# Moving small steps inside an engine's program: chain work, a cast, and long GpSimd additions in a fused attention and feed-forward kernel

## The chip, the core and the metric

The kernel runs on one core of a Trainium2 chip. The core has five engines that run their own instruction streams and wait for each other through semaphores: TensorE (PE, matrix products and transposes into PSUM), VectorE (DVE), ScalarE (ACT), GpSimd (POOL) and SyncE (SP, which issues the transfers). The metric is the device time of one execution in microseconds; lower is better.

## The reference, cut to what matters

The input x has 4 batches of 2048 rows of 256. Four residual layers follow each other, each on a layer norm of x:

```python
x = x + attn_a(layernorm(x))   # linear attention, 16 heads of 16, bias
x = x + ffn(layernorm(x))      # shared expert: square(relu(z @ Ws1)) @ Ws2, plus routed experts
x = x + attn_b(layernorm(x))   # iterated softmax over the first 16 positions of each batch
x = x + ffn(layernorm(x))
```

In `attn_a`, q and k pass through elu + 1, `kv = k^T v` is summed over a whole batch, and `out = (q kv) / max(q . sum(k), 1e-6)`. In `attn_b` only the first 16 rows of each batch attend (64 rows in all, three iterations with a test for an early end); every other row gets the bias `ob` alone. The routed part of `ffn` is weighted by the truncated softmax of two values, which is zero unless the router weights are very large, so the kernel guards it with a flag that is off for these inputs.

## The kernel before

All rows are cut into 16 groups of 512 (4 tiles of 128). **Pass 1** (up to about 182 us of the span) normalises each group, forms k and q in split precision (high and low fp32r halves) and sums `kv` for each batch. **Pass 2** is a software pipeline of 18 steps, written out by hand for each engine in a function `step(g, b)`. In step i three groups are in work at once: group i gets the attention, group r = i - 1 the first feed-forward layer, group v = i - 2 the second. The program order of each engine, and nothing else, decides what runs next; an instruction that waits holds up all that stands behind it on its engine.

The names used from here on, in the order of TensorE's step before the change, with their lines:

- **W** (L1539): q times kv and Wo, 16 products into PA. VectorE adds the result to x (**W add**, L1071).
- **bc** (L1407): spreads 1/normalizer of group i + 1 over its heads into PB; VectorE multiplies q by it (**q_scale**, L956). It reads `n_op`, written by VectorE (**n_split**, L949).
- **f1** (L1557): first layer's hidden product of group r; ScalarE squares its relu (L751, L753).
- **f4** (L1522): output product of the second layer, group v. VectorE adds two of its tiles to x, each scaled by its row's 1/variance (**scaled_sum**, L1059); ScalarE scales the other two (L738), and GpSimd adds them (**y3 add**, L549).
- **r2** (L1571): spreads the inverse variances of group r over columns of PT. VectorE makes them (L1049, one reciprocal for groups r and v together) from what GpSimd prepared (`four_variances`, L494 to L501) from VectorE's `bn_stats` (**x_stats**, L1038).
- **T2** (L1577): transposes of group i.
- **f3** (L1586): hidden product of the second layer. It reads `h2s`, the product of the squared relu and r2's columns, made by VectorE (**h2s**, L1095).
- **n** (L1398): normalizer of group i + 2. VectorE takes it out of PSUM (L939), inverts it (L941) and casts it to its high half (L943, `n_hi`); n_split makes the operand with the low half.
- **f2** (L1522 again): output product of the first layer; VectorE adds it to x (**f2 add**, L1104), after GpSimd has added the rows `ob` there (**ob add**, L455).

The 64 special rows of `attn_b` are carried along as a serial **chain** of small pieces, `chain(i, slot)`, with slots 1, 2 and 3 at fixed places of each engine's step. Most pieces pass a result from one engine to the next.

Of the kernel before, what the change touches and what calls it, by code (L numbers as in the profile page):

```python
# [44 lines left out]
def hybrid_kernel(nc, x_in, Wq, bq, Wk, bk, Wv, bv, Wo, bo, qw, qb, kw, vw, vb, ow, ob,  # L45
# [18 lines left out]
    with ExitStack() as ctx:  # L64
# [16 lines left out]
        minus_low = sb("minus_low", [P, 1])  # L81
# [165 lines left out]
        bn3, var3, rsq = sem("bn3"), sem("var3"), sem("rsq")  # L247
# [9 lines left out]
        n_mm, n_taken, n_inv, n_op_done = [sem(n) for n in ("n_mm", "n_taken", "n_inv", "n_op_done")]  # L257
# [73 lines left out]
        def _(sp):  # L331
# [74 lines left out]
            sp.wait_ge(stored, 16 * (NG - 1))  # L406
# [9 lines left out]
        def _(pool):  # L416
# [114 lines left out]
            def step(g, b):  # L531
                i = g * B + b
                r, nr, _ = lagged(g, b, 1)
                v, nv, _ = lagged(g, b, 2)
                if runs(r):
# [3 lines left out]
                ge(pool, rsq, i - 1)  # L539
                if runs(v):  # L540
                    four_variances(1, v, bn3, var3)
# [20 lines left out]
        def _(act):  # L562
# [40 lines left out]
            def pass1(b, last):  # L603
                for g in range(G):
# [5 lines left out]

                    ge(act, q_done, n)
# [121 lines left out]
            def scale_tiles(i, v):  # L733
                act.wait_ge(f4_mm, v + 1)
                act.wait_ge(rsq, i)
# [5 lines left out]
            def step(g, b):  # L741
# [4 lines left out]
                if i == 0:  # L746
                    fold_ffn()
                if runs(r):
# [7 lines left out]
                chain(i, 1)  # L756
# [8 lines left out]
                chain(i, 2)  # L765
                if i <= NG:
                    run_experts(i, r)
# [16 lines left out]
        def _(dve):  # L784
# [45 lines left out]
            nc.vector.memset(minus_low[:, :], -1.0).then_inc(sel_ready, 1)  # L830
# [40 lines left out]
            def pass1(b, last):  # L871
                for g in range(G):
# [4 lines left out]

                    ge(dve, g_mm, n)
# [11 lines left out]
                    if last and g == G - 1:  # L890
                        dve.wait_ge(sel_ready, 2 + T + 1)
                        n_take(0)
                        n_split(0)
# [9 lines left out]
                    if isinstance(n, int) and n == 2:  # L903
                        dve.wait_ge(sel_ready, 2)
                        for t in range(T):
                            nc.vector.memset(minus_low[t * 2 * H:t * 2 * H + H, :], 0.0).then_inc(sel_ready, 1)
                        by_half = ident[:, :].rearrange("p (t u k o) -> p t u k o", t=T, u=2, o=1)
                        nc.vector.tensor_tensor(sel[:, :, :].rearrange("p k f -> p (k f)").rearrange("p (t k e) -> p t k e", t=T, e=HD),
                                                by_half[:, :, 0, :, :].to_broadcast([P, T, H, HD]),
                                                by_half[:, :, 1, :, :].to_broadcast([P, T, H, HD]), ALU.add).then_inc(sel_ready, 1)  # L910
# [25 lines left out]
            def n_take(j):  # L936
# [5 lines left out]
                dve.wait_ge(n_inv, 2 * j + 1)  # L942
                nc.vector.tensor_copy(n_hi[:, :], n_sb[:, :]).then_inc(n_inv, 1)  # L943

            def n_split(j):

                dve.wait_ge(n_inv, 2 * j + 2)
# [92 lines left out]
            def reciprocal_variances(i, r, v):  # L1040

                slots = slice(0 if runs(r) else 1, 2 if runs(v) else 1)
                if runs(r):
                    dve.wait_ge(var2, 5 * (r + 1))
                    ge(dve, r2_mm, r)
                if runs(v):
                    dve.wait_ge(var3, 5 * (v + 1))
                    ge(dve, f4_scaled, 2 * v)
                nc.vector.reciprocal(ln_rsq[:, slots, :], ln_a[:, slots, :]).then_inc(rsq, 1)  # L1049

            def scaled_sum(i, v, nv):
# [3 lines left out]
                dve.wait_ge(rsq, i)  # L1055
# [6 lines left out]
            def step(g, b):  # L1062
# [3 lines left out]
                j, nj, _ = lagged(g, b, -1)  # L1066
                if runs(i):
# [13 lines left out]
                if i > 0:  # L1081
                    reciprocal_variances(i, r, v)
# [4 lines left out]
                if runs(v):  # L1087
                    scaled_sum(i, v, nv)
                chain(i, 1)
                if runs(r):  # L1090
# [4 lines left out]
                    nc.vector.tensor_tensor(h2s, h2, PT[:, 1, :], ALU.mult).then_inc(f1_scaled, 1)  # L1095
                chain(i, 2)
                if runs(i + 2):
                    n_take(i + 2)
                chain(i, 3)
# [5 lines left out]
                if runs(i + 2):  # L1105
                    n_split(i + 2)
                if runs(r):
# [163 lines left out]
        def _(pe):  # L1271
# [138 lines left out]
            def pass1(b, last):  # L1410
                for g in range(G):
# [3 lines left out]
                    if last and g == G - 1:  # L1415
                        n_product(0, 0, 0)
# [108 lines left out]
            def step(g, b):  # L1525
# [22 lines left out]
                if runs(j):  # L1548
                    ge(pe, f2_added, i - 1)
                    bc_product(j, PB)  # L1550
                if runs(r):
# [13 lines left out]
                chain(i, 1)  # L1565
                if runs(r):
                    pe.wait_ge(rsq, i)
                    pe.wait_ge(n_taken, min(i + 2, NG))
                    ge(pe, f1_scaled, r)
                    for t in range(T):  # L1570
                        last = nc.tensor.transpose(PT[:, 1, t * P:(t + 1) * P], ln_rsq[:, 0, t:t + 1].to_broadcast([P, P]), ident[:, :])  # L1571
                    last.then_inc(r2_mm, 1)
# [10 lines left out]
                chain(i, 2)  # L1583
# [5 lines left out]
                chain(i, 3)  # L1589
                if runs(r):  # L1590
# [5 lines left out]
                    down(PB, h2s, f2_mm)  # L1596
                if i <= NG:
# [162 lines left out]
```

## Time and profile before

| what | value |
|---|---|
| time, median of 3 runs | 439.25 us (438.79 to 441.06) |
| the profiled execution, its own time | 441.03 us |
| its span, first to last instruction | 439.2 us |
| mean granted TensorE clock | 0.986 |
| busy share: PE, DVE, ACT, POOL | 92%, 71%, 47%, 49% |

The profile is of one execution. Times in it are in microseconds from the start of the span. PE's busy time is modelled for overlapping products, so the share says that PE is rarely without work, not that it runs at its peak.

### The profile page before, as it was taken

Reading aid. Unit: us, or ns where it says so; the run is one execution under the profiler, and the core shown is the slowest. Engines: PE = TensorE matmul, PEld = TensorE weight load, DVE = VectorE, ACT = ScalarE, POOL = GpSimd, SP = SyncE. Lnnn points to the kernel's source line nnn. Section 1 sums busy time; section 2 is a strip of 40 time slices with the busy share of each in tenths; the row PEclk is TensorE's granted clock in tenths of the full one; section 3 lists DMA queues with packets and bytes.
Section 4 is the critical chain, followed back from the end, with each engine's and each line's share of the span. In section 5 each row is a group of like instructions: output and inputs, shape, how many; then the busy total and the mean of one; then the engine's idle time right before and its main releaser. Section 6 shows DMA issues by size and latency. Waiting matters only on the chain.

```text
span 439.2 us, 7483 instructions
## 1 busy us (share of the span) xinstructions
PE 404.7 (92%) x2458; PEld 322.7 (73%) x2458; DVE 313.5 (71%) x654; ACT 204.5 (47%) x354; POOL 217.2 (49%) x315
## 2 busy tenths in 40 slices
PE   8898999999999998989989989999899999969983
PEld 5787889988988896777866767677666676747752
DVE  6779976576668666474667688797768877977644
ACT  3766686778778775033324422222342144223340
POOL 3675775776677664032144514662441744533630
PEclk9999999999999999899999999999999999989998
DMA  8701211111100000400011101101110110110022
GB/s 269 236 16 35 80 65 48 49 48 48 48 0 0 1 1 1 99 3 0 6 54 51 52 5 50 52 1 50 49 51 0 51 53 1 50 49 29 22 91 64
DMA packets 22982, 20.64 MB, mean 47 GB/s; under 512 B 3398, under 2 KB 22924, under 8 KB 22924
## 3 DMA queue, kind: packets, MB, share of 16 engines
q1 hardware_dynamic: 22364, 19.40, 14.1%
q8 instruction: 29, 0.48, 0.4%
q10 hardware_dynamic: 560, 0.52, 0.4%
q14 instruction: 29, 0.24, 0.2%
HBM read 11.33 MB, written 8.45 MB: 45 GB/s over the span
## 4 chain that ended last, share of the span: by engine, by line
PE 57%; DVE 18%; ACT 8%; issue 8%; POOL 7%; DVEq 1%; POOLq 0%; ACTq 0%
PE PB L1522 12%; PE PA L1539 11%; PE PT L1557 6%; PE PT L1586 4%; PE PB L1407 3%; ACT scratch L567 3%; PE PG L1358 3%; POOL ln_rstd L444 2%; DVE x_all L1059 2%; ACT scratch L614 2%; POOL ln_rstd L442 2%; DVE ln_bn L797 2%; DVE scratch L1095 2%; ACT xn_pair L578 2%; PE PT L1398 2%
## 5 line engine op out<-in xcount | busy, mean ns | idle before, releaser
L494 POOL TENSOR_TENSOR ln_a<-ln_bn 128x4 f32<-128x4 f32 x32 | 6.7, 210 | 124.2 <-DVE ln_bn L1038 124.2
L1522 PE MATMUL PB<-ws,scratch 128*128 128x256 f32 x248 | 62.3, 395 | 1.9 <-issue 1.9
L1522 PEld LDWEIGHTS PB<-ws,scratch 128*128 128x128 f32 x248 | 46.1, 195 | 20.1 <-issue 14.8
L1539 PE MATMUL PA<-kvwo,q_all 128*128 128x256 f32 x256 | 57.9, 379 | 0.0
L751 ACT ACTIVATE scratch<-PT 128x512 f32<-128x512 f32 x16 | 9.6, 598 | 102.2 <-PE PT L1557 102.2
L1539 PEld LDWEIGHTS PA<-kvwo,q_all 128*128 128x128 f32 x256 | 48.5, 190 | 6.5
L466 POOL TENSOR_TENSOR xn_pair<-scratch,xn_pair 128x1024 fp32r<-128x1024 f32 x16 | 38.5, 2406 | 20.3 <-ACT xn_pair L578 20.3
L882 DVE SCALAR_TENSOR_TENSOR scratch<-scratch,PB 128x512 f32<-128x512 f32 x32 | 20.9, 684 | 38.6 <-ACT scratch L614 38.6
L1038 DVE BATCH_NORM_STATS2 ln_bn<-x_all 128x6 f32<-128x256 f32 x128 | 44.1, 406 | 0.1
L567 ACT ACTIVATE scratch<-x_all,ln_shift,ln_rstd 128x255 f32 (+1 forms) x60 | 31.1, 593 | 22.6 <-POOL ln_shift L448 22.5
L455 POOL TENSOR_TENSOR x_all<-x_all,wvo 128x1024 f32 (+1 forms) x16 | 38.6, 2410 | 0.1
L455 POOL TENSOR_TENSOR x_all<-x_all,ob_rows 128x1024 f32<-128x1024 f32 x16 | 38.1, 2381 | 0.9 <-PE PA L1577 0.7
L1331 PE MATMUL PB<-wk_hi,xt_hi 128*128 128x256 f32 x128 | 36.9, 288 | 0.5 <-DVE xt_lo L825 0.4
L1358 PE MATMUL PG<-xn_pair,k_hi 128*128 128x512 f32 x128 | 35.2, 419 | 1.1 <-ACT k_hi L622 1.1
L1333 PE MATMUL PB<-wk_hi,xt_lo 128*128 128x256 f32 x128 | 36.2, 283 | 0.0
L1332 PE MATMUL PB<-wk_lo,xt_hi 128*128 128x256 f32 x128 | 36.2, 283 | 0.0
L1557 PE MATMUL PT<-scratch,ffn_weights 128*128 128x512 f32 x64 | 30.8, 603 | 0.0
L1104 DVE TENSOR_TENSOR x_all<-PB,x_all 128x1024 f32<-128x1024 f32 x16 | 19.5, 1221 | 15.2 <-PE PB L1522 15.2
L1586 PE MATMUL PT<-scratch,ffn_weights 128*128 128x512 f32 x32 | 18.8, 670 | 11.4 <-DVE scratch L1095 11.3
L1071 DVE TENSOR_TENSOR x_all<-PA,x_all 128x1024 f32<-128x1024 f32 x16 | 19.5, 1219 | 12.5 <-PE PA L1539 12.5
L1358 PEld LDWEIGHTS PG<-xn_pair,k_hi 128*128 128x128 f32 x128 | 24.0, 195 | 6.0 <-issue 1.3
L442 POOL TENSOR_SCALAR ln_rstd<-ln_mv 128x4 f32<-128x4 f32 x16 | 12.2, 764 | 31.4 <-DVE ln_mv L800 27.9
(252 smaller groups left out, 943.0 us busy)
## 6 DMA issues: line engine op xcount, KB each, us to landing
x_all<-n_L_attn_a_inputs_q_dram SPq DMA_DIRECT2D x15, 512.0 KB, 3.6
out_dram<-x_all SPq DMA_DIRECT2D x15, 512.0 KB, 3.2
out_dram<-x_all SPq DMA_DIRECT2D x2, 256.0 KB, 2.2
x_all<-n_L_attn_a_inputs_q_dram SPq DMA_DIRECT2D x2, 128.0 KB, 3.0
x_all<-n_L_attn_a_inputs_q_dram ACTq DMA_DIRECT2D x2, 128.0 KB, 3.4
setup<-in_L_attn_a_Wk_dram SPq DMA_DIRECT2D x1, 256.0 KB, 4.9
setup<-in_L_attn_a_Wq_dram ACTq DMA_DIRECT2D x1, 256.0 KB, 5.1
wvo<-in_L_attn_a_Wv_dram SPq DMA_DIRECT2D x1, 256.0 KB, 6.4
```

The source lines that it names most:

```text
L455: nc.gpsimd.tensor_tensor(x_group(n), x_group(n), rows_[:, :].rearrange("p (o d) -> p o d", o=1).to_broadcast([P, T, D]), ALU.add).then_in ...
L466: nc.gpsimd.tensor_tensor(xn_pair[:, :, 1, :], xn[g % 2], xn_pair[:, :, 0, :].bitcast(F32), ALU.subtract).then_inc(x_lo, 1)
L567: nc.scalar.activation(dst[:, t:t + 1, 0:width], x_tile(n, t)[:, :, 0:width], ACT.Identity, scale=ln_rstd[:, slot, t:t + 1], bias=ln_shift ...
L1038: nc.vector.bn_stats(ln_bn[:, slot, t:t + 1, :], x_tile(n, t)).then_inc(bn, 1)
L1331: mm(dst, hi, wk_hi[:, c, :], start=(c == 0), stop=False)
L1332: mm(dst, hi, wk_lo[:, c, :], start=False, stop=False)
L1333: last = mm(dst, lo, wk_hi[:, c, :], start=False, stop=(c == C - 1))
L1358: mm(PG[:, c, :], k_hi[:, t, c * P:(c + 1) * P], xn_pair[:, t, :, :].rearrange("p h d -> p (h d)"), start=(g == 0 and t == 0), stop=False, ...
L1522: last = mm(four(pair)[:, t, :], h[:, t * P:(t + 1) * P], ws2[:, :], start=True, stop=True)
L1539: last = mm(four(PA)[:, t, :], q_all[:, n * C + c, t * P:(t + 1) * P], kvwo[:, b * C + c, :], start=(c == 0), stop=(c == C - 1))
L1557: last = mm(PT[:, 0, :], w1c[:, c, :], x2t[:, c, :], start=(c == 0), stop=(c == C - 1))
L1586: mm(PT[:, 0, :], wc, h2s, start=False, stop=True, skip_group_check=True).then_inc(f3_mm, 1)
```

## The change

The change reorders the steps of pass 2 and a little of pass 1, and moves one cast between engines.

- TensorE: slot 1 of the chain and r2 go ahead of f1; slot 2 goes ahead of T2 (from step 2 on); slot 3 goes behind f2. The normalizer product of group 0 goes ahead of the last group's k product in pass 1.
- VectorE: the reciprocal is cut in two, for group r ahead of the W add, and for group v behind q_scale. Slot 1 goes ahead of x_stats, h2s ahead of scaled_sum, slot 3 behind n_split. The cast to `n_hi` leaves VectorE.
- ScalarE: makes `n_hi` (`n_high`), ahead of the second layer's relu. Slot 1 goes ahead of the first layer's relu.
- GpSimd: the y3 add is one step later (group u = i - 3), and it and the ob add stand at the head of the step, behind a wait for the normalizer product of the step before.
- SyncE: the store of a finished group is one step later too.

```diff
@@ SyncE step
+                u, nu, _ = lagged(g, b, 3)
+                if runs(u):
+                    sp.wait_ge(out_dve, 2 * (u + 1))
+                    sp.wait_ge(out_pool, u + 1)
+                    sp.dma_start(out_dram[bass.ds(nu, 1)].rearrange("o p t d -> p (o t) d"), x_group(nu)).then_inc(stored, 16)
...
-                elif runs(v):
-                    sp.wait_ge(out_dve, 2 * (v + 1))
-                    sp.wait_ge(out_pool, v + 1)
-                    sp.dma_start(out_dram[bass.ds(nv, 1)].rearrange("o p t d -> p (o t) d"), x_group(nv)).then_inc(stored, 16)
...
-            sp.wait_ge(stored, 16 * (NG - 1))
+            sp.wait_ge(stored, 16 * (NG - 2))
@@ GpSimd step
+                if runs(r):
+                    pool.wait_ge(n_mm, min(i + 2, NG))
+                if runs(u):
+                    pool.wait_ge(f4_scaled, 2 * (u + 1))
+                    last = x_all[:, nu * T + 2:(nu + 1) * T, :]
+                    nc.gpsimd.tensor_tensor(last, last, y3, ALU.add).then_inc(out_pool, 1)
...
-                if runs(v) and v < NG - 1:
-                    pool.wait_ge(f4_scaled, 2 * (v + 1))
-                    last = x_all[:, nv * T + 2:(nv + 1) * T, :]
-                    nc.gpsimd.tensor_tensor(last, last, y3, ALU.add).then_inc(out_pool, 1)
@@ ScalarE
+            def n_high(j):
+
+                act.wait_ge(n_inv, j + 1)
+                ge(act, n_op_done, j)
+                nc.scalar.activation(n_hi[:, :], n_sb[:, :], ACT.Copy).then_inc(n_hi_done, 1)
...
+                if runs(i + 2):
+                    n_high(i + 2)
@@ VectorE
-                dve.wait_ge(n_inv, 2 * j + 1)
-                nc.vector.tensor_copy(n_hi[:, :], n_sb[:, :]).then_inc(n_inv, 1)
...
-                nc.vector.scalar_tensor_tensor(n_op[:, :], n_hi[:, :].bitcast(F32), minus_low[:, 0:1], n_sb[:, :],
-                                               ALU.mult, ALU.add).then_inc(n_op_done, 1)
+                nc.vector.scalar_tensor_tensor(n_op[:, :], n_sb[:, :], low_row[:, 0:1], n_hi[:, :].bitcast(F32),
+                                               ALU.mult, ALU.subtract).then_inc(n_op_done, 1)
...
+                if runs(r):
+                    reciprocal_variances(0, r, var2, r2_mm, rsq)
...
-                if i > 0:
-                    reciprocal_variances(i, r, v)
+                if runs(v):
+                    reciprocal_variances(1, v, var3, f4_scaled, rsq3)
+                chain(i, 1)
@@ TensorE
+                if isinstance(n, int) and n == NG - 1:
+                    n_product(0, 0, 0)
```

The selection matrix `sel` changes sign to fit the new `n_op`. Three places of the new order follow. The first is VectorE in step 13, from the W add to the f2 add; the rows L1236 to L1242 are the chain's slot 1, L1247 its slot 2 and L1250 its slot 3. Before:

```order
L1071 TENSOR_TENSOR x_all<-PA,x_all 128x1024
L956 TENSOR_TENSOR q_all<-q_all,PB 128x1024
L1049 RECIPROCAL ln_rsq<-ln_a 128x8
L1038 BN_STATS ln_bn<-x_all 128x6 x4
L1059 SCALAR_TENSOR_TENSOR x_all<-PB,ln_rsq,x_all 128x256 x2
L1236 TENSOR_REDUCE b_weights<-q_all 128x16
...
L1242 TENSOR_SCALAR b_weights<-b_weights,q_all 128x256
L1095 TENSOR_TENSOR scratch<-scratch,PT 128x512
L1247 TENSOR_TENSOR b_weights<-PG,b_weights 128x256
L939 TENSOR_SCALAR n_sb<-PT 128x128
L941 RECIPROCAL n_sb<-n_sb 128x128
L943 CAST n_hi<-n_sb 128x128
```

And the same stretch of the changed program, where L1103 is h2s, L1067 scaled_sum, L1051 x_stats and L1246 to L1252 slot 1:

```order
L1057 RECIPROCAL ln_rsq<-ln_a 128x4
L1081 TENSOR_TENSOR x_all<-PA,x_all 128x1024
L969 TENSOR_TENSOR q_all<-q_all,PB 128x1024
L1057 RECIPROCAL ln_rsq<-ln_a 128x4
L1246 TENSOR_REDUCE b_weights<-q_all 128x16
...
L1252 TENSOR_SCALAR b_weights<-b_weights,q_all 128x256
L1051 BN_STATS ln_bn<-x_all 128x6 x4
L1103 TENSOR_TENSOR scratch<-scratch,PT 128x512
L1067 SCALAR_TENSOR_TENSOR x_all<-PB,ln_rsq,x_all 128x256 x2
L1257 TENSOR_TENSOR b_weights<-PG,b_weights 128x256
L954 TENSOR_SCALAR n_sb<-PT 128x128
L956 RECIPROCAL n_sb<-n_sb 128x128
```

h2s stood behind scaled_sum and slot 1; now slot 1 stands ahead of x_stats, and scaled_sum behind h2s. The second place is TensorE in step 7, from bc to f2; L1660 is the chain's slot 1 and L1602 its slot 3. Before:

```order
L1407 MATMUL PB<-n_op,sel 128x128 x8
L1557 MATMUL PT<-scratch,ffn_weights 128x512 x2
L1522 MATMUL PB<-ws,scratch 128x256 x4
L1660 MATMUL PG<-q_all,scratch 128x256 x4
L1571 MATMUL PT<-ident,ln_rsq 128x128 x4
L1577 MATMUL PA<-ident,x_all 128x128 x8
L1586 MATMUL PT<-scratch,ffn_weights 128x512
L1398 MATMUL PT<-q_all,kmask 32x128 x8
L1602 MATMUL PG<-ident,q_all 128x128 x2
L1522 MATMUL PB<-ws,scratch 128x256 x4
```

And after, with L1673 and L1615 for the two chain pieces, L1567 for r2, L1575 for f1, L1599 for f3 and L1410 for n:

```order
L1419 MATMUL PB<-n_op,sel 128x128 x8
L1673 MATMUL PG<-q_all,scratch 128x256 x4
L1567 MATMUL PT<-ident,ln_rsq 128x128 x4
L1575 MATMUL PT<-scratch,ffn_weights 128x512 x2
L1532 MATMUL PB<-ws,scratch 128x256 x4
L1589 MATMUL PA<-ident,x_all 128x128 x8
L1599 MATMUL PT<-scratch,ffn_weights 128x512
L1410 MATMUL PT<-q_all,kmask 32x128 x8
L1532 MATMUL PB<-ws,scratch 128x256 x4
L1615 MATMUL PG<-ident,q_all 128x128 x2
```

Slot 1 and r2 moved from behind f4 to the place ahead of f1, and slot 3 from ahead of f2 to the end of the step. The third place is the end of pass 1 on TensorE, where the k product of the last group is 24 rows L1331 to L1333 (L1343 to L1345 after) and the q product begins with L1346 (L1358 after). Before:

```order
L1358 MATMUL PG<-xn_pair,k_hi 128x512 x8
L1363 MATMUL PG<-xn_pair,k_lo 128x256 x8
L1331 MATMUL PB<-wk_hi,xt_hi 128x256
L1332 MATMUL PB<-wk_lo,xt_hi 128x256
L1333 MATMUL PB<-wk_hi,xt_lo 128x256
...
L1398 MATMUL PT<-q_all,kmask 32x128 x8
L1346 MATMUL PA<-xt_hi,wq_hi 128x512
```

And after:

```order
L1370 MATMUL PG<-xn_pair,k_hi 128x512 x8
L1375 MATMUL PG<-xn_pair,k_lo 128x256 x8
L1410 MATMUL PT<-q_all,kmask 32x128 x8
L1343 MATMUL PB<-wk_hi,xt_hi 128x256
L1344 MATMUL PB<-wk_lo,xt_hi 128x256
L1345 MATMUL PB<-wk_hi,xt_lo 128x256
...
L1358 MATMUL PA<-xt_hi,wq_hi 128x512
```

The normalizer product of group 0 moved from behind the last k product to the place ahead of it.

## Rows read from the trace of the kernel before

**Rows 1.** Page, busy time and share of the span, by engine.

```profile
PE 404.7 (92%) x2458; PEld 322.7 (73%) x2458; DVE 313.5 (71%) x654; ACT 204.5 (47%) x354; POOL 217.2 (49%) x315
```

**Rows 2.** Chain that ended last, step 4: start us, us, engine, tile, line.

```profile
239.70 3.45 PE PA L1539 x16
243.15 0.84 PE PB L1407 x8
243.99 1.77 PE PT L1557 x4
245.76 1.86 PE PB L1522 x8
...
247.64 0.88 DVE x_all L1059 x2
248.52 0.60 DVE scratch L1095
...
249.17 1.12 PE PT L1586 x2
250.29 0.57 PE PT L1398 x16
250.87 1.92 PE PB L1522 x8
252.79 3.45 PE PA L1539 x16
```

**Rows 3.** Waits of PE, whole span: us in total, times, longest us.

```profile
PE PT L1586 <- DVE scratch L1095: 11.3, 11, 3.4
PE PT L1407 <- DVE n_op L949: 2.6, 1, 2.6
PE PB L1522 <- issue: 1.9, 4, 0.7
...
PE PG L1602 <- ACT q_all L704: 1.5, 1, 1.5
...
PE PB L1407 <- DVE n_op L949: 1.0, 3, 0.4
...
PE PG L1638 <- ACT b_weights L690: 0.6, 1, 0.6
```

**Rows 4.** Windows: stretch, length, busy per engine, granted clock, DMA share, GB/s.

```profile
177.40:181.00 3.60, 3.60 (x11) 2.82 (x11) 1.29 (x2) 0.00 (x0) 0.00 (x0) 0.53 0.18 1
...
389.00:391.90 2.90, 2.89 (x18) 0.99 (x18) 0.29 (x1) 0.85 (x2) 0.00 (x0) 0.52 0.00 0
...
426.70:430.10 3.40, 3.40 (x10) 2.68 (x9) 0.00 (x0) 1.32 (x2) 0.00 (x0) 0.50 0.48 158
...
437.00:438.00 1.00, 0.00 (x0) 0.00 (x0) 0.00 (x0) 0.00 (x0) 0.00 (x0) 0.50 0.99 327
```

**Rows 5.** Timeline of DVE, step 11 and step 13: start, length, instruction.

```profile
346.66 1.31 DVE L949 SCALAR_TENSOR_TENSOR n_op<-n_hi,minus_low,n_sb 128x128 fp32r<-128x128 f32 x1
...
386.02 2.21 DVE L1242 TENSOR_SCALAR b_weights<-b_weights,q_all 128x256 f32<-128x256 f32 x1
```

**Rows 6.** Timeline of POOL, the same two stretches.

```profile
345.28 2.54 POOL L455 TENSOR_TENSOR x_all<-x_all,ob_rows 128x1024 f32<-128x1024 f32 x1
...
384.50 1.28 POOL L549 TENSOR_TENSOR x_all<-x_all,scratch 128x512 f32<-128x512 f32 x1 [0.30 <-ACT scratch L738]
385.73 2.35 POOL L455 TENSOR_TENSOR x_all<-x_all,ob_rows 128x1024 f32<-128x1024 f32 x1
```

**Rows 7.** Timeline of ACT, a 128x128 activation from SBUF to SBUF.

```profile
418.60 0.31 ACT L715 ACTIVATE q_all<-q_all 128x128 f32<-128x128 f32 x1
```

**Rows 8.** Page, costliest groups: busy us, mean ns of one, idle before.

```profile
L751 ACT ACTIVATE scratch<-PT 128x512 f32<-128x512 f32 x16 | 9.6, 598 | 102.2 <-PE PT L1557 102.2
...
L1038 DVE BATCH_NORM_STATS2 ln_bn<-x_all 128x6 f32<-128x256 f32 x128 | 44.1, 406 | 0.1
...
L1071 DVE TENSOR_TENSOR x_all<-PA,x_all 128x1024 f32<-128x1024 f32 x16 | 19.5, 1219 | 12.5 <-PE PA L1539 12.5
```

More of the change, by code:

```diff
@@ L256, in hybrid_kernel @@
         kvwo_mm, kvwo_done, sel_ready = [sem(n) for n in ("kvwo_mm", "kvwo_done", "sel_ready")]
-        n_mm, n_taken, n_inv, n_op_done = [sem(n) for n in ("n_mm", "n_taken", "n_inv", "n_op_done")]
+        n_mm, n_taken, n_inv, n_hi_done, n_op_done = [sem(n) for n in ("n_mm", "n_taken", "n_inv", "n_hi_done", "n_op_done")]
         bc_mm, q_scaled, w_mm, w_added = [sem(n) for n in ("bc_mm", "q_scaled", "w_mm", "w_added")]
@@ L609, in pass1 @@
                     x_high(n, g)
+                    if last and g == G - 1:
+                        n_high(0)
                     ge(act, q_done, n)
@@ L746, in step @@
                 if i == 0:
+                    n_high(1)
                     fold_ffn()
+                chain(i, 1)
                 if runs(r):
@@ L755, in step @@
                     scale_tiles(i, v)
-                chain(i, 1)
                 if runs(i):
@@ L876, in pass1 @@
                         copy_g(b - 1)
+                    if last and g == G - 1:
+                        dve.wait_ge(sel_ready, 2 + T + 1)
+                        n_take(0)
+                        n_split(0)
                     ge(dve, g_mm, n)
@@ L889, in pass1 @@
                     nc.vector.tensor_tensor(k_lo[:, :, :], k_tok, k_hi[:, :, :].bitcast(F32), ALU.subtract).then_inc(k_lo_done, 1)
[L890 to L893, printed above, removed]
                     if not (last and g == G - 1):
@@ L905, in pass1 @@
                         for t in range(T):
-                            nc.vector.memset(minus_low[t * 2 * H:t * 2 * H + H, :], 0.0).then_inc(sel_ready, 1)
+                            nc.vector.memset(low_row[t * 2 * H:t * 2 * H + H, :], 0.0).then_inc(sel_ready, 1)
                         by_half = ident[:, :].rearrange("p (t u k o) -> p t u k o", t=T, u=2, o=1)
                         nc.vector.tensor_tensor(sel[:, :, :].rearrange("p k f -> p (k f)").rearrange("p (t k e) -> p t k e", t=T, e=HD),
-                                                by_half[:, :, 0, :, :].to_broadcast([P, T, H, HD]),
-                                                by_half[:, :, 1, :, :].to_broadcast([P, T, H, HD]), ALU.add).then_inc(sel_ready, 1)
+                                                by_half[:, :, 1, :, :].to_broadcast([P, T, H, HD]),
+                                                by_half[:, :, 0, :, :].to_broadcast([P, T, H, HD]), ALU.subtract).then_inc(sel_ready, 1)
                     if last and g == G - 1:
@@ L1038, in x_stats, with reciprocal_variances @@
                     nc.vector.bn_stats(ln_bn[:, slot, t:t + 1, :], x_tile(n, t)).then_inc(bn, 1)
[L1040 to L1049, printed above, removed]
+            def reciprocal_variances(slot, j, ready, used, done):
+                dve.wait_ge(ready, 5 * (j + 1))
+                ge(dve, used, j if slot == 0 else 2 * j)
+                nc.vector.reciprocal(ln_rsq[:, slot, :], ln_a[:, slot, :]).then_inc(done, 1)
             def scaled_sum(i, v, nv):
@@ L1054, in scaled_sum @@
                 dve.wait_ge(f4_mm, v + 1)
-                dve.wait_ge(rsq, i)
+                dve.wait_ge(rsq3, v + 1)
                 if v < B:
@@ L1080, in step @@
                     q_scale(j, nj, PB)
-                if i > 0:
-                    reciprocal_variances(i, r, v)
+                if runs(v):
+                    reciprocal_variances(1, v, var3, f4_scaled, rsq3)
+                chain(i, 1)
                 if runs(i):
@@ L1086, in step @@
                     x_stats(n, 0, bn2)
-                if runs(v):
-                    scaled_sum(i, v, nv)
-                chain(i, 1)
                 if runs(r):
@@ L1095, in step @@
                     nc.vector.tensor_tensor(h2s, h2, PT[:, 1, :], ALU.mult).then_inc(f1_scaled, 1)
+                if runs(v):
+                    scaled_sum(i, v, nv)
                 chain(i, 2)
@@ L1098, in step @@
                     n_take(i + 2)
-                chain(i, 3)
                 if runs(r):
@@ L1106, in step @@
                     n_split(i + 2)
+                chain(i, 3)
                 if runs(r):
@@ L1414, in pass1 @@
                     k_product(n, g, b)
-                    if last and g == G - 1:
-                        n_product(0, 0, 0)
                     if isinstance(n, int) and n == 0:
@@ L1550, in step @@
                     bc_product(j, PB)
+                chain(i, 1)
+                if runs(r):
+                    pe.wait_ge(rsq, r + 1)
+                    pe.wait_ge(n_taken, min(i + 2, NG))
+                    ge(pe, f1_scaled, r)
+                    for t in range(T):
+                        last = nc.tensor.transpose(PT[:, 1, t * P:(t + 1) * P], ln_rsq[:, 0, t:t + 1].to_broadcast([P, P]), ident[:, :])
+                    last.then_inc(r2_mm, 1)
                 if runs(r):
@@ L1564, in step @@
                     down(PB if v < NG - 1 else PA, h3, f4_mm)
[L1565 to L1572, printed above, removed]
+                if i > 1:
+                    chain(i, 2)
                 if runs(i):
@@ L1582, in step @@
                     pe.wait_ge(kvwo_done, B)
-                chain(i, 2)
+                if i <= 1:
+                    chain(i, 2)
                 if runs(r):
@@ L1588, in step @@
                     n_product(jj, njj, bjj)
-                chain(i, 3)
                 if runs(r):
@@ L1596, in step @@
                     down(PB, h2s, f2_mm)
+                chain(i, 3)
                 if i <= NG:
```

13 lines of the change are left out of this document (7 added, 6 removed).

## The prediction

> **What bounds the kernel.** I read the busy shares first: PE is busy for 92% of the span [rows 1], so what can be won is PE's idle time and the time that PE runs at the lower clock. Next comes the chain that ended last, in an ordinary step without chain work [rows 2]. W, bc, f1 and f4 follow each other on PE; then the chain leaves PE for scaled_sum (0.88) and h2s (0.60) and comes back to PE for f3, n and f2. From one W start to the next it is 252.79 - 239.70 = 13.09 us. f4 ends at 247.62 and f3 starts at 249.17, a hole of 1.55 us which r2 and T2 fill but for 0.25. By their counts, 4 and 8 transposes, these take about 0.44 and 0.87. An ordinary step is thus 12.84 us of PE work. Then I read who makes PE wait [rows 3]: h2s for 11.3 us at 11 places, of which 3.4 at one; n_op for 2.6 at the end of pass 1 and 1.0 at three places after; f4, four times and 1.9 in all, put down to "issue", which I take for its wait on q_scale; a chain piece on ScalarE for 1.5. Last, the clock: behind the long waits the windows show a granted clock of 0.53, 0.52 and 0.50, the lower level of 1.2 GHz, for some 3 us each [rows 4].
>
> **Why VectorE is late.** At 386.02 a VectorE instruction on SBUF operands takes 2.21 us and ends 0.15 us after GpSimd's ob add, which runs from 385.73 to 388.08; n_split at 346.66 takes 1.31 us and ends at 347.97, with GpSimd's addition ending at 347.82 [rows 5, 6]. So a VectorE instruction whose operands are all in SBUF stands still until a long GpSimd addition has ended. Additions with a PSUM operand beside it keep their length (W adds average 1.22 over all steps) [rows 8].
>
> **The change, part by part.** I write E for the end of W and lay out a new ordinary step from these durations. PE: bc to E+0.84, r2 to 1.28, f1 to 3.05, f4 to 4.91, T2 to 5.78, f3 to 6.90, n to 7.47, f2 to 9.39; the next E is 12.84 [rows 2]. VectorE: W add and q_scale (1.2 each) to E+2.5, reciprocal, x_stats (44.1 us for 128, so 1.4 for four) to about 4.0. f1's square is ready 1.45 us after f1 (two activations of 0.60 and gaps), at 4.5, so h2s ends at 5.2 [rows 2, 8]. f3 wants to start at 5.78, so **its wait is gone, with 0.6 us to spare**. The cast on ScalarE costs about 0.31 [rows 7]. It holds the second relu back until after the inversion, but that result is wanted only by f4 of the next step, over 5 us later.
>
> GpSimd starts behind n, at 7.47: y3 add 1.28 and ob add 2.35 end at about 11.2 [rows 6]. n_split wants to start at 10.7, behind the f2 add, so it is held in every step, to about 11.6; x_stats then ends at 12.9 and the next reciprocal at 13.1, where r2 wants it at 12.84 + 0.84 = 13.7. The hold costs nothing as long as it grows by less than 0.6 us.
>
> 1. **End of pass 1.** n_op is ready while PE is in the q product, so bc does not wait: 2.6 us [rows 3]. The stretch behind it, 177.4 to 181, ran at 0.53 [rows 4], and 3.6 x 0.47 = 1.7 us goes too if PE keeps busy. What is late next is the last group's q_scale, and it gives W a wait of about 0.2. I take **4.1** (2.6 if the clock drops all the same; 4.3).
> 2. **h2s waits, 11.3 us** [rows 3]. The chain's slot 1 (three to six operations on 256 columns or fewer; at x_stats's 0.34 to 0.41 each I estimate 1.0 to 1.8 us) now lies ahead of x_stats, and only what goes beyond the 0.6 us shows: 0.4 left in step 2 and 0.5 in step 13. In step 16, which has no W, T2 or n as cover, 1.4 us of wait stays or changes place. I take **9.0** (5.6 if step 13 keeps its 3.4; 10.4).
> 3. **Clock behind step 13's wait**: 2.9 x 0.48 = **1.4** [rows 4] (0 to 1.4).
> 4. **bc and q_scale waits**, 0.6 of the 1.0 and the 1.9 [rows 3]. They came from chain work and held casts between n and the next W. Two slot 3 pieces (the softmax in steps 10 and 12, three operations on 256 columns, estimated at 0.41 each as x_stats's [rows 8], 1.3 us with links) still delay the W add of the next step, by 0.35 and 0.2. Gain **1.9** (1.2 to 2.5).
> 5. **Step 8's wait of 1.5** for the softmax's exp: slot 3 on PE is now behind f2, and the held subtraction ahead of it runs before GpSimd starts. **1.5** (1.0 to 1.7).
> 6. **Step 1 loses.** Its chain piece stood between f1 and T2 and covered the path f1, square, h2s (1.45 + 0.60 + 0.05 = 2.1). Now only T2's 0.87 covers it, which is 1.25 us of new wait; the 0.6 for L1638 goes [rows 3]. **-0.65** (-0.3 to -1.0).
> 7. **Step 0 loses** about **0.4**: n_high stands ahead of ScalarE's fold copies, for which bc waits (0 to -0.6).
> 8. **Step 16: 0** (+1.5 to -1.5). r2 now precedes f1, and the reciprocal for it stands behind the f2 add and x_stats (1.2 + 1.35): PE starts f1 about 2.9 us later than before. It saves r2's and part of f3's later waits. Before, f2 of this step ran at 0.50 [rows 4]. If the clock falls in the new hole, this is lost again; if not, 1 us or so is won.
> 9. **End of the kernel.** The store of group 14 (512 KB) used to be out before the last two halves. Now it is issued behind the four small output stores, just ahead of those halves. At the 327 GB/s that the last store reached [rows 4] 512 KB is 1.6 us; a part of it passes before the first half is ready. **-1.2** (0 to -1.6).
>
> On the last term, the Trainium skill, DMA: Bandwidth & Descriptors, section Queues, rings and completion order, says that each DMA engine takes descriptors of one issuer's ring in order; by that the halves queue behind the late store and the whole 1.6 us would show. No row of the trace before has two large stores together.
>
> Sum: 4.1 + 9.0 + 1.4 + 1.9 + 1.5 - 0.65 - 0.4 + 0 - 1.2 = **15.65 us**. The profiled execution took 441.03 (span 439.2) and would take 425.4. It lies 1.8 us above the median of the runs shown; from the median 439.25 I get **423.6 us**.
>
> **Rivals.**
>
> *VectorE becomes the bound.* In every step n_split stands behind both long GpSimd additions. Were GpSimd 1 us later than I place it (its own additions were stretched where VectorE was busy in SBUF: 2.54 against 2.35 [rows 6]), the reciprocal would come at 14.1 where r2 wants it at 13.7, and each of 13 steps would lose 0.4 to 0.5, some 6 us: 429.6. For it: slack is only 0.6. Against: n's removal of the cast frees VectorE, and no other pure SBUF instruction falls under the additions. The Trainium skill, SBUF - State Buffer, section SBUF: two separate sides, has a rule that speaks so: VectorE, with two SBUF inputs, and GpSimd take a shared port pair for a whole instruction, whichever comes first, and the other stands still. By that rule the hold can go either way.
>
> *Step 13 keeps its wait.* Its six chain operations still precede h2s. If they are held as at 386.02, terms 2 and 3 lose 3.4 + 1.4: 428.4. Against: in the new order GpSimd has only short operations there.
>
> *Slower.* r2 is now ahead of f1, and every piece of PE's step is behind it. If VectorE's reciprocal came later than E+0.84 by more than (15.65 + 2.2)/13 = 1.4 us in each of 13 steps, the change would cost over 2 us: about 443. That needs the held n_split to end 2 us later than I place it, which only a GpSimd that starts late could do.
>
> *The change does not do what it says*: waits reappear one for one at the moved places, as in terms 6 to 9. Then about 438 to 440.
>
> **Chances.** My forecast with its small variations, 417.5 to 427: 0.67. VectorE bound: 0.14. Step 13 keeps its wait: 0.10. No change: 0.03. Slower: 0.06. The likeliest is 423.6; the range reaches from term bounds at the low side (all good ends give some 21 us, 418 to 419) to both middle rivals with a little more, 418.5 to 431. A difference of 0.5%, about 2.2 us, is what these runs can tell from none. Faster by more than that 0.91, within it 0.03, slower 0.06.
>
> **What would show it.** PE's waits for h2s fall from 11.3 to under 4 us. bc has no wait at the end of pass 1, and W first starts near 177.7. Ordinary steps come every 12.85 us; step 13 takes about 14.6, and the granted clock is 1.00 all through it. n_split is long (0.8 or more) in most steps while its cast is gone. A wait of 1.2 for h2s appears in step 1, one of 2 to 3 us ahead of r2 in step 16. The last store lands some 1.2 us later behind the last scaled_sum. I am wrong if r2 waits in ordinary steps, or if new chain waits stand ahead of f1.

## The result and the profile after

The changed kernel takes **417.05 us** (median of 4 runs, 414.62 to 417.81) against 439.04 us for the kernel before, measured beside it (4 runs). The ratio is 0.948, 95% interval 0.943 to 0.953. Ratios here and below leave out runs that are more than 1.5% above the fastest of the same kernel. The direction and the mechanism were forecast, the size was not: 423.6 us was predicted with a range of 418.5 to 431.0, and the time lies below it. The profiled execution took 417.81 us with a span of 416.1, so it gained 23.1 us of span where the sum said 15.65. Between the medians the gain is 22.0; the profiled execution of the kernel before took 2.0 more than its median here.

I read PE's waits first, as [rows 3] were read: us in total, times, longest.

```profile
PE PT L1599 <- DVE scratch L1103: 1.2, 1, 1.2
...
PE PT L1567 <- DVE ln_rsq L1057: 1.0, 1, 1.0
PE PB L1419 <- ACT ffn_weights L733: 0.8, 1, 0.8
PE PG L1741 <- ACT q_all L727: 0.7, 1, 0.7
```

f3's wait for h2s has fallen from 11.3 us at 11 places [rows 3] to 1.2 at one, the one forecast in step 1. Of the others, r2 (L1567) and the chain piece L1741 wait in step 16, and bc (L1419) in step 0. In steps 2 to 14 no wait is shown any more. Next, PE's timeline of one ordinary step, step 4 (start us, length, instruction). It is best read by the distance from one start to the next, since the lengths overlap.

```profile
233.30 3.62 PE L1549 MATMUL PA<-kvwo,q_all 128*128 128x256 f32 x16
236.57 1.19 PE L1419 MATMUL PB<-n_op,sel 128*128 128x128 f32 x8
237.60 0.62 PE L1567 MATMUL PT<-ident,ln_rsq 128*128 128x128 f32 x4
238.05 1.88 PE L1575 MATMUL PT<-scratch,ffn_weights 128*128 128x512 f32 x4
239.77 1.89 PE L1532 MATMUL PB<-ws,scratch 128*128 128x256 f32 x8
241.50 1.04 PE L1589 MATMUL PA<-ident,x_all 128*128 128x128 f32 x8
242.37 1.02 PE L1599 MATMUL PT<-scratch,ffn_weights 128*128 128x512 f32 x2
243.32 0.64 PE L1410 MATMUL PT<-q_all,kmask 128*32 128x128 f32 x16
243.90 1.99 PE L1532 MATMUL PB<-ws,scratch 128*128 128x256 f32 x8
245.73 0.81 PE L1549 MATMUL PA<-kvwo,q_all 128*128 128x256 f32 x3
```

The step takes 245.73 - 233.30 = 12.43 us; I had forecast 12.84. The same view of the kernel before, from f1 to n of step 4, with VectorE's q_scale beside it, shows where that 0.4 us lay:

```profile
243.83 1.93 PE L1557 MATMUL PT<-scratch,ffn_weights 128*128 128x512 f32 x4
...
244.33 1.21 DVE L956 TENSOR_TENSOR q_all<-q_all,PB 128x1024 f32<-128x1024 f32 x1
...
245.64 1.96 PE L1522 MATMUL PB<-ws,scratch 128*128 128x256 f32 x8
247.44 0.60 PE L1571 MATMUL PT<-ident,ln_rsq 128*128 128x128 f32 x4
247.88 1.04 PE L1577 MATMUL PA<-ident,x_all 128*128 128x128 f32 x8
249.17 1.12 PE L1586 MATMUL PT<-scratch,ffn_weights 128*128 128x512 f32 x2 [0.25 <-DVE scratch L1095]
250.22 0.64 PE L1398 MATMUL PT<-q_all,kmask 128*32 128x128 f32 x16
```

From start to start, before and after: f1 to what follows 1.81 and 1.72; f4 to what follows 1.80 and 1.73; T2 to f3 1.29 and 0.87; f3 to n 1.05 and 0.95. The sum of the differences is 0.09 + 0.07 + 0.42 + 0.10 = 0.68, the whole gain of the step (13.10 to 12.43, within rounding). The idle time that the row shows is 0.25.

By the first W product of each step in the two traces, the gain lies here (us):

| stretch | before | after | gain | predicted |
|---|---|---|---|---|
| start to the first W | 181.76 | 177.40 | 4.36 | 4.1 |
| steps 0 and 1 | 29.97 | 30.89 | -0.92 | -1.05 |
| steps 2 to 12 and 14 | 175.30 | 161.38 | 13.92 | 8.5 |
| step 13 | 19.91 | 13.78 | 6.13 | 5.3 |
| step 15 to the end | 32.26 | 32.65 | -0.39 | -1.2 |

The prediction's terms are not given by step: 5.3 is 19.91 less the 14.6 forecast for step 13, and 8.5 is what the sum leaves beside the other rows. Most of the 7.5 us that were missed is thus in the steady steps, in which PE does the same work in another order.

### The profile page after: what moved, and what is told of

Same layout as the page of the kernel before. It is cut to its first block, busy times and chain, and to the rows that moved or that the text cites. A ratio compares the mean times of both kernels' runs of the same rounds, so it can differ in the third digit from the quotient of the medians.

```text
span 416.1 us, 7524 instructions
## 1 busy us (share of the span) xinstructions
PE 396.5 (95%) x2458; PEld 320.4 (77%) x2458; DVE 307.3 (74%) x653; ACT 207.7 (50%) x370; POOL 216.6 (52%) x315
## 4 chain that ended last, share of the span: by engine, by line
PE 65%; DVE 9%; ACT 8%; POOL 7%; issue 7%; DMA 1%; DVEq 1%; POOLq 0%; ACTq 0%; SPq 0%
PE PB L1532 13%; PE PA L1549 13%; PE PT L1575 6%; PE PT L1599 4%; PE PA L1589 3%; ACT scratch L571 3%; PE PB L1419 3%; PE PG L1370 3%; POOL ln_rstd L445 2%; POOL ln_rstd L443 2%; DVE ln_bn L812 2%; PE PT L1410 2%; ACT scratch L620 2%; ACT xn_pair L582 2%; PE PT L1567 2%
## 5 line engine op out<-in xcount | busy, mean ns | idle before, releaser
L1532 PE MATMUL PB<-ws,scratch 128*128 128x256 f32 x248 | 60.5, 387 | 0.0
L1051 DVE BATCH_NORM_STATS2 ln_bn<-x_all 128x6 f32<-128x256 f32 x128 | 44.5, 409 | 0.2
L1343 PE MATMUL PB<-wk_hi,xt_hi 128*128 128x256 f32 x128 | 37.0, 289 | 0.5 <-DVE xt_lo L840 0.4
L1345 PE MATMUL PB<-wk_hi,xt_lo 128*128 128x256 f32 x128 | 36.2, 283 | 0.0
L1370 PE MATMUL PG<-xn_pair,k_hi 128*128 128x512 f32 x128 | 33.7, 405 | 1.1 <-ACT k_hi L628 1.1
L1575 PE MATMUL PT<-scratch,ffn_weights 128*128 128x512 f32 x64 | 31.5, 616 | 0.0
L542 POOL TENSOR_TENSOR x_all<-x_all,scratch 128x512 f32<-128x512 f32 x15 | 19.0, 1268 | 21.2 <-PE PT L1410 14.9
L1370 PEld LDWEIGHTS PG<-xn_pair,k_hi 128*128 128x128 f32 x128 | 23.1, 188 | 5.6 <-issue 1.3
```

The source lines that it names most:

```text
L1051: nc.vector.bn_stats(ln_bn[:, slot, t:t + 1, :], x_tile(n, t)).then_inc(bn, 1)
L1343: mm(dst, hi, wk_hi[:, c, :], start=(c == 0), stop=False)
L1345: last = mm(dst, lo, wk_hi[:, c, :], start=False, stop=(c == C - 1))
L1370: mm(PG[:, c, :], k_hi[:, t, c * P:(c + 1) * P], xn_pair[:, t, :, :].rearrange("p h d -> p (h d)"), start=(g == 0 and t == 0), stop=False, ...
L1532: last = mm(four(pair)[:, t, :], h[:, t * P:(t + 1) * P], ws2[:, :], start=True, stop=True)
L1575: last = mm(PT[:, 0, :], w1c[:, c, :], x2t[:, c, :], start=(c == 0), stop=(c == C - 1))
```

## The experiments

The theory after the result (A): a wait of PE costs more than its idle time in the trace, and a wait shorter than the end of the products before it shows no idle time at all. The main rival (B): r2's new place is in itself the shorter order. The edits below are shortened; a name such as h2s or r2 stands for its lines.

**VectorE's order undone alone.** In the changed kernel:

```diff
-                h2s (waits f1_sq, r2_mm)
                 if runs(v):
                     scaled_sum(i, v, nv)
+                h2s (waits f1_sq, r2_mm)
```

> The changed kernel, with h2s put back behind scaled_sum on VectorE and nothing else undone. Theory A (a wait of PE costs more than the idle time that the trace shows beside it: about 0.17 us of the products before it still count as busy, and the first product behind it takes 0.10 longer): f3 waits for h2s again in nearly every step, the start of T2 to the start of f3 grows from 0.87 to about 1.8 us while the wait shown is 0.6 to 0.7, f3 to n grows from 0.95 to 1.05, and a step takes 13.4 instead of 12.43; time 428 to 431. Rival B (what was under-sized is the gain of r2's new place ahead of f1): f3's wait comes back with what the row shows and no more, a step takes about 13.0, time 423 to 425.

Measured: 426.68 us, ratio to before 0.970 (0.965 to 0.974). Timeline of an ordinary step; PEld is the weight load.

```profile
243.62 1.04 PE L1589 MATMUL PA<-ident,x_all 128*128 128x128 f32 x8
...
245.35 0.30 PEld L1599 LDWEIGHTS PT<-scratch,ffn_weights 128*128 128x128 f32 x2 [0.93 <-DVE scratch L1105]
245.35 1.12 PE L1599 MATMUL PT<-scratch,ffn_weights 128*128 128x512 f32 x2 [0.69 <-DVE scratch L1105]
...
246.41 0.64 PE L1410 MATMUL PT<-q_all,kmask 128*32 128x128 f32 x16
```

T2 to f3 is 1.73 (0.87 without the wait), f3 to n 1.06 (0.95), and the step is 13.38. The wait costs 0.96 where the row shows 0.69. The two missing parts can be seen. T2 counts as busy for 1.04 us though f3 follows it after 0.87 when nothing waits, so 0.17 of a wait lies under it. And the weight load starts together with the product that waited; in the changed kernel it starts at 242.26, 0.11 ahead of its product at 242.37:

```profile
242.26 0.30 PEld L1599 LDWEIGHTS PT<-scratch,ffn_weights 128*128 128x128 f32 x2
```

The Trainium skill, TensorE: Matmul & The Clock Gate, section Step-by-step: what each phase is for, says that weight loads are pulled ahead of running products and that the end of one product overlaps the beginning of the next, which one standing alone can't use. The trace agrees where nothing waits; ahead of the waiting product the load was not pulled ahead. The total came 1.3 us below my 428, since the chain's steps lose less (some of their pieces already fill the hole).

**PE's order undone alone.** r2 back behind f4, in the changed kernel:

```diff
                 chain(i, 1)
-                r2 (waits rsq, n_taken)
                 f1
                 f4
+                r2 (waits rsq, n_taken)
                 if i > 1:
                     chain(i, 2)
```

> The changed kernel, with r2 alone put back behind f4 on PE (ahead of T2). Theory A: h2s is still ahead of scaled_sum and is ready when T2 ends, so f3 waits for little or nothing; the starts of f1, f4, r2 and T2 stay 1.72, 1.73 and 0.45 apart, a step takes 12.4 to 12.6 and the time is 416 to 420; step 16, where r2 no longer waits ahead of f1, gains 1 to 2 us. Rival B (r2's place made the ordinary step shorter): f1 to f4 is 1.81 and f4 to r2 1.80 as before the change, a step takes 12.8 or more, time 421 or more.

Measured: 418.14 us, 0.950 (0.945 to 0.954): 1.1 above the changed kernel, which the intervals don't separate. But the ordinary step takes 12.81 with no wait shown, as B said, and A's numbers for it were wrong; the time lies in A's range (416 to 420) and not in B's (421 or more). Timeline of one:

```profile
238.34 1.93 PE L1568 MATMUL PT<-scratch,ffn_weights 128*128 128x512 f32 x4
...
238.84 1.21 DVE L969 TENSOR_TENSOR q_all<-q_all,PB 128x1024 f32<-128x1024 f32 x1
...
240.15 1.97 PE L1532 MATMUL PB<-ws,scratch 128*128 128x256 f32 x8
...
241.95 0.60 PE L1581 MATMUL PT<-ident,ln_rsq 128*128 128x128 f32 x4
...
242.39 1.04 PE L1589 MATMUL PA<-ident,x_all 128*128 128x128 f32 x8
...
242.65 0.69 DVE L1103 TENSOR_TENSOR scratch<-scratch,PT 128x512 f32<-128x512 f32 x1 [1.22 <-issue]
...
243.39 1.13 PE L1599 MATMUL PT<-scratch,ffn_weights 128*128 128x512 f32 x2
```

q_scale ends at 240.05 and f4 starts 0.10 behind it, where f1 alone would have let it start at 238.34 + 1.72 = 240.06. h2s ends at 243.34 and f3 starts at 243.39, where T2 would have let it start at 243.26. Both are waits of about 0.1 without idle time in the trace. That made a second form of A: r2's place matters only since it shifts f4 away from q_scale and brings h2s forward. (That the total hardly moves: step 1 is shorter by 0.43, and the stretch from step 15's W to the end, with f1 of step 16 no longer behind r2's wait, by 2.1.)

**r2 issued twice** tells this second form from B: four more transposes ahead of f1 on top of the last kernel.

```diff
                 chain(i, 1)
+                r2 (the same four transposes to PT, without its count)
                 f1
                 f4
                 r2
```

> The kernel of the run with r2 behind f4, which issues r2 a second time ahead of f1 (the same four transposes to the same place; work is added, none is left out). It shifts f1 and f4 by 0.45 without moving r2. Theory A, second form (the place of r2 matters only because f4 came 0.1 us after q_scale's end and f3 0.1 after h2s: waits that show no idle time since the products before them still drain): f1 to f4 falls from 1.81 to 1.72, f4 to r2 from 1.80 to 1.73, and an ordinary step takes 12.85 to 13.0. Rival B (r2 behind f4 is in itself the slower order): both stay at 1.81 and 1.80, and a step takes 13.25.

Measured: 423.94 us (one run). One of its ordinary steps:

```profile
239.60 1.88 PE L1574 MATMUL PT<-scratch,ffn_weights 128*128 128x512 f32 x4
241.32 1.89 PE L1532 MATMUL PB<-ws,scratch 128*128 128x256 f32 x8
243.05 0.60 PE L1587 MATMUL PT<-ident,ln_rsq 128*128 128x128 f32 x4
```

f1 to f4 is 1.72 and f4 to r2 1.73 with r2 still behind f4: B falls. The step takes 13.10, above my 12.85 to 13.0, because h2s still waits for the late r2: T2 to f3 stays at 1.00 and f3 to n at 1.05. 12.43 + 0.44 for the transposes + 0.13 + 0.10 is 13.10.

Since a copy of r2 stands ahead of f1 in this run too, it leaves open whether f1 and f4 are shorter only behind r2. The trace of the kernel before answers that in step 15, which has no bc and no q_scale:

```profile
410.39 1.88 PE L1557 MATMUL PT<-scratch,ffn_weights 128*128 128x512 f32 x4
412.11 1.89 PE L1522 MATMUL PB<-ws,scratch 128*128 128x256 f32 x8
413.83 0.60 PE L1571 MATMUL PT<-ident,ln_rsq 128*128 128x128 f32 x4
```

f1 to f4 and f4 to r2 are 1.72 each, with r2 behind f4 and none of it ahead of f1.

**h2s first, in the kernel before**, one part of the change alone:

```diff
+                h2s (waits f1_sq, r2_mm)
                 scaled_sum(i, v, nv)
                 chain(i, 1)
-                h2s (waits f1_sq, r2_mm)
```

> The kernel before, with h2s ahead of scaled_sum and of the chain's slot 1 on VectorE, and nothing else of the change. Theory A: that swap alone takes away the wait of the ordinary steps with what it really costs (0.67 us in a step where 0.25 is shown) and the 3.4 of step 13 with the half clock behind it: an ordinary step takes 12.45 to 12.65, time 424 to 428. Rival B (it takes r2's place, the spread slots or GpSimd's new order as well): a step stays above 12.8, step 13 keeps a wait over 2 us, time 431 or more.

Measured: 441.33 us (median of 10 runs, 437.21 to 444.50), ratio 1.002 (0.999 to 1.006): nothing. Its waits of PE:

```profile
PE PG L1602 <- DVE q_all L1155: 2.8, 1, 2.8
...
PE PG L1602 <- DVE q_all L1215: 2.2, 2, 1.1
PE PB L1407 <- DVE n_op L949: 2.0, 2, 1.6
```

The ordinary step is 12.81 (steps 2 and 4; 13.36 in step 3), B's figure, and step 13 has lost its wait, as A had it. But A's time was far off. h2s waits for r2 behind f4, slot 1 and all of VectorE's later work waits with it, and PE then stands ahead of the chain pieces and of bc: the waits at L1602 add up to 11.8 us, as much as the 11.3 for h2s before.

**Slot 1 undone alone**, in the changed kernel on VectorE:

```diff
-                chain(i, 1)
                 x_stats(n, 0, bn2)
                 h2s
                 scaled_sum(i, v, nv)
+                chain(i, 1)
```

> The changed kernel with VectorE's chain slot 1 alone put back behind scaled_sum (h2s stays ahead of both; PE's slots stay as changed). Theory A (the slots had to move with h2s: PE's piece between f4 and T2, wanted 8.2 to 9 us after the step's start, reads what VectorE's slot 1 makes, which then ends 2 us or more later): in six or seven of the steps 5 to 14 PE waits 1 to 3 us ahead of that piece, ordinary steps stay at 12.43; time 424 to 431. Rival B (h2s ahead of scaled_sum and r2 ahead of f1 carry the gain alone, the spread slots are worth little): chain steps grow by less than 0.3 each, time 416.5 to 420.

Measured: 434.08 us, 0.983 (0.978 to 0.988): 17 us worse than the changed kernel (15 by the ratios to the kernel before), more than A's 424 to 431. Ordinary steps stay at 12.43.

```profile
PE PG L1615 <- DVE b_weights L1267: 2.5, 1, 2.5
...
PE PG L1615 <- DVE q_all L1200: 2.2, 1, 2.2
```

PE waits 1.5 to 2.5 us ahead of a chain piece in six steps (6, 8, 9, 10, 12 and 15), and behind the 2.2 the granted clock fell: 0.66 from 273 to 278, which makes step 6 19.72 long. So h2s's place pays only together with slot 1's: here PE's pieces of the chain stand at their new places, and VectorE makes what they read too late.

**The end of pass 1 alone**, in the kernel before: the product, take and split of group 0's normalizer early (the diff of the change).

> The kernel before, with the first n product, its take and its split ahead of the last group of pass 1 and nothing else. By the trace after the change this is worth 4.4 us (the first W started at 177.40 instead of 181.76): W first starts at 177.3 to 177.8 and the time is 434 to 435.5. Rival: the rest needs the cast on ScalarE, and W starts at 179 or later, time 436.5 or more.

Measured: 437.74 us, 0.996 (0.993 to 0.998). The first W starts where I said, but the time is above my 434 to 435.5. The window (granted clock in the third column from the end) shows a loss in step 2 of the profiled execution:

```profile
177.23 3.69 PE L1539 MATMUL PA<-kvwo,q_all 128*128 128x256 f32 x16 [1.19 <-DVE q_all L956]
```

```profile
219.60:223.60 4.00, 4.00 (x25) 3.12 (x25) 1.47 (x3) 1.32 (x2) 0.43 (x1) 0.57 0.20 64
```

Behind the same wait of 1.87 for h2s in step 2 the clock fell here, and step 2 took 16.34 instead of 14.71; in the trace of before it stayed at 1.00 behind a wait of 1.86 (223.0 to 226.4). But from step 15's W on this execution took 30.60 us instead of 32.29, so that against the trace of before the whole 4.5 is left (a span of 434.7 for 439.2). The medians, 437.74 and 439.65, differ by 1.9; what the other executions lost, and where, no trace shows.

**The cast back on VectorE**, in the changed kernel:

```diff
                 nc.vector.reciprocal(n_sb, n_sb).then_inc(n_inv, 1)
+                nc.vector.tensor_copy(n_hi, n_sb).then_inc(n_hi_done, 1)
@@ ScalarE
-                n_high(i + 2)
```

> The changed kernel with the cast of n back on VectorE, between the reciprocal and the f2 add, instead of on ScalarE. Theory A (a VectorE cast on SBUF operands stands still under GpSimd's additions, which now start right behind n): the cast takes 1 to 2.5 us instead of 0.25, the f2 add, x_stats and the W add behind it come 1 us or more later, f4 waits for q_scale in ordinary steps; a step takes 12.8 to 13.6, time 422 to 432. Rival B (the cast slips in between the two additions, or its delay is hidden): steps stay at 12.4 to 12.5, time 416.5 to 418.5.

Measured: 424.48 us, 0.966 (0.964 to 0.968). An ordinary step takes 13.17:

```profile
232.79 2.35 POOL L456 TENSOR_TENSOR x_all<-x_all,ob_rows 128x1024 f32<-128x1024 f32 x1
232.83 2.39 DVE L953 CAST n_hi<-n_sb 128x128 fp32r<-128x128 f32 x1
...
238.06 0.65 PE L1564 MATMUL PT<-ident,ln_rsq 128*128 128x128 f32 x4 [0.22 <-DVE ln_rsq L1054]
```

The cast (0.25 by itself) stands until the ob add has ended, the f2 add behind it starts at 235.14 instead of 233.50, and bc, r2 and f4 wait (f1 to f4 takes 1.80 again). A is borne out.

**GpSimd's additions at their old places**, in the changed kernel (the store stays one step late):

```diff
-                pool.wait_ge(n_mm, min(i + 2, NG))
-                y3 add of group u
                 add_row(nr, ob_rows, ob_added)
...
                 four_variances(0, i, bn2, var2)
+                y3 add of group v
```

> The changed kernel with GpSimd's two long additions back at their old places: ob add first thing in GpSimd's step without waiting for n, y3 add of the same step's group behind the variances. Theory A (the additions' place decides how long VectorE is held; it was needed for the gain): x_stats or n_split are held on the path, r2 or h2s comes late, time 421 or more. Rival B (with the cast gone from VectorE the old places hold nothing that PE waits for): ordinary steps stay at 12.4 to 12.5, time 415.5 to 418.5, with the store of group 14 no longer behind its late addition.

Measured: 417.46 us, 0.948 (0.944 to 0.951), the changed kernel's time, and 12.43 an ordinary step. n_split is not held here (0.34 us, 0.75 in the changed kernel), and nothing is won by it. Once the cast has left VectorE, the place of the additions is worth nothing that can be measured.

**The three losses mended**, in the changed kernel:

```diff
-                chain(i, 1)
-                r2
+                if i not in (1, NG): chain(i, 1)
+                if i < NG: r2
                 f1
+                if i in (1, NG): chain(i, 1)
                 f4
+                if i == NG: r2
@@ SyncE: the store of group 14, ahead of the four small output stores
-                if runs(u): store of group u
+                if runs(u) and u < NG - 2: store of group u
+                if v == NG - 2: store of group v
```

> The changed kernel with its three losses mended: in step 1 the chain piece behind f1 instead of ahead of r2; in step 16 the order f1, chain piece, f4, r2; the store of group 14 issued ahead of the four small output stores. By the traces: step 1 14.1 instead of 15.31 (1.2 us), step 16 without the wait of 0.99 ahead of r2, the 0.71 ahead of the chain piece and the half clock behind them (2.5 to 3.2 us), the tail from the last variances to the end 6.1 instead of 7.0 (0.9 us): time 411.5 to 413.5. Rival: the clock falls in step 16 all the same, or the wait for h2s only changes place, and the last stores are not what ends the kernel: 414.5 to 417.

Measured: **412.24 us** (412.06 to 412.57, 5 runs), 0.938 (0.936 to 0.940), faster than both kernels. PE's timeline in step 16, then SyncE's at the end:

```profile
393.30 1.88 PE L1583 MATMUL PT<-scratch,ffn_weights 128*128 128x512 f32 x4
395.02 0.59 PE L1753 MATMUL PG<-ws,q_all 128*128 128x256 f32 x2
395.45 1.89 PE L1536 MATMUL PB<-ws,scratch 128*128 128x256 f32 x8
```

```profile
399.64 0.38 SPq L378 DMA_DIRECT2D out_dram<-x_all  x1
404.80 1.76 SPq L413 DMA_DIRECT2D out_dram<-q_all  x4
406.83 1.19 SPq L382 DMA_DIRECT2D out_dram<-x_all  x2
```

The same two stretches of the changed kernel, the first by its window (f1 and the start of f4):

```profile
397.90:401.00 3.10, 3.10 (x6) 1.25 (x5) 0.49 (x2) 0.00 (x0) 0.59 (x3) 0.57 0.01 3
```

```profile
409.02 2.02 SPq L409 DMA_DIRECT2D out_dram<-q_all  x4
411.15 0.40 SPq L374 DMA_DIRECT2D out_dram<-x_all  x1
411.61 1.52 SPq L378 DMA_DIRECT2D out_dram<-x_all  x2
```

Step 1 falls from 15.31 to 13.82 (1.5). From step 15's W to the first operation behind the last x_stats is 22.6 instead of 25.6 us (3.0): f1 takes 1.72 from its start to the next where it took 3.05 at a granted clock of 0.57. The last two halves, from their issue to the end of the span, take 410.2 - 406.83 = 3.4 us instead of 416.1 - 411.61 = 4.5, and from the start of the last f4 to the end of the span it is 8.8 instead of 10.0: the late store cost 1.2 by this run. In the kernel before the same stretch took 9.1, so against that it cost 0.9.

## Why the prediction was right in direction and wrong in size

- **The step that failed is "An ordinary step is thus 12.84 us of PE work".** It took the hole between f4 and f3 and counted only the 0.25 that shows as idle; the term mis-sized is the cost of h2s's and q_scale's waits per step (terms 2 and 4). The shortest step measured has 12.43 us. The other 0.42 were waits too: f4 for q_scale (0.09 and 0.07 behind it) and the parts of f3's wait that lie under T2 (0.17) and in the weight load that starts late (0.10). The runs with h2s behind scaled_sum, with r2 behind f4 and with r2 twice showed each of these come and go. I also had f4 wait for q_scale only at the four places with an "issue" entry [rows 3]; it waited in the ordinary step as well. That 12.43 holds no wait at all is not shown: f2 to W takes 1.83 wherever f2 stands right behind n, and 1.73 in steps 5 and 8 of the kernel before, where a chain piece stands between.
- **Size.** Over steps 2 to 12 this is about 11 x 0.42 = 4.6 of the 5.4 us missed in steps 2 to 12 and 14, an estimate from the ordinary step. The 0.4 of wait that I left in step 2 did not come either. In step 13 I forecast 14.6 with 0.5 of wait; it took 13.78, of which 0.42 is the same error and the rest that wait, which is gone. What little remains I have not assigned. The good ends of all terms add up to 21.5 us (the prediction says some 21), still less than the 22.0 between the medians: the missing share stood in no term.
- **Right:** the end of pass 1 (4.36 for 4.1; the run with it alone puts W at 177.23), the losses of steps 0 and 1 (-0.92 for -1.05) and, nearly, the late store (0.9 against the kernel before and 1.2 against the run that mends it, for 1.2). The Trainium skill, DMA: Bandwidth & Descriptors, section Queues, rings and completion order, would by the prediction's reading have made the last of these 1.6; the runs show less.
- **Step 16** was given 0 and came out so: from the end of step 15's last product to the start of the last f4 it takes 11.2 us for 11.1. f3's wait of 1.38 no longer shows, but r2's grew from 0.59 to 0.99, slot 1 waits 0.71 ahead of it, and f1 ran at half clock in the new hole, as f2 had before [rows 4]. The 0.5 that the stretch from step 15's W to the last f4 won (22.62 for 23.14) lies in step 15.
- **The rivals.** VectorE did not become the bound: n_split is held (0.75 for 0.34), but the reciprocal ends at 236.79 and r2 starts at 237.60, so 0.8 us was spare. The run with the cast back shows how near it was: 2.39 us of cast use that up and cost 7 us in all. Step 13 did not keep its wait, and no wait came back one for one in the changed kernel; with h2s first alone, they did. The reading behind both of these rivals, that a VectorE instruction with all its operands in SBUF stands still under a long GpSimd addition, was too broad. In the kernel before, the reciprocal of n, from SBUF to SBUF, takes its usual 0.95 us from 251.26 on while the ob add runs from 249.79 to 252.15; it is n_split, the cast and L1242 that were seen to stand.
- **What each part was worth.** h2s's place (about 10 us by the run without it) and slot 1's on VectorE (15 to 17, with PE's pieces left at their new places) only work together: h2s first in the old order gives nothing. The cast is worth 7, the end of pass 1 2 to 4, r2's place 2.6 in steps 2 to 14, most of it lost again in step 1 (0.4) and from step 15's W on (2.1); GpSimd's new order is worth nothing. The places of slots 2 and 3 were not tried apart.

## What to carry to other kernels

Measure a step of TensorE by the distance from one start to the next, and compare it with the shortest distance that the same pair of instructions has anywhere in the trace: what lies above it at the same clock is probably a wait, even where the row shows no idle time; a run that moves one neighbour tells. An instruction moved ahead of others on one engine only helps if what its successors read is moved with it; trace each result one engine further before counting the wait as gone. And look at the ends of a pipeline apart from its steady steps: an order that is best where all stages run (r2 ahead of f1) cost 2 us where some are missing.

## What the runs showed that was not expected

- A wait of 0.1 us ahead of f4 or f3 shows no idle time and costs about 0.2 us with what follows it; one of 0.69 shown costs 0.96.
- The lower clock is no fixed price of a wait. In step 16, r2's wait of 0.98 or 0.99 behind the chain's 0.71 is in six of the traces here; behind it f1 took 3.05, 3.20 and 3.37 us to the next start (the changed kernel, h2s behind scaled_sum, GpSimd's old places) and 1.72 in the other three (the cast on VectorE, r2 twice, slot 1 late). The mended kernel, without that hole, spreads over 0.5 us in five runs, the changed one over 3.2 in four. That the clock makes this difference is not shown. Of the changed kernel's runs the longest, 417.81, had a mean granted clock of 0.991 and the shortest, 414.62, had 0.995, but 417.15 had 0.995 as well.
